# A rebuilt attention stage in a tokenizer, attention and expert kernel: two 34-row projections side by side, decays moved, rows normalised after the gather

## The reference

```python
# tok: frame differences, embedding, smoothing forwards and backwards (alpha 0.1), a linear layer
x_diff = concat([0, xt[:, 1:] - xt[:, :-1]])
x_emb = einsum('btc,dc->btd', x_diff, W_ve) + b_ve
h = ((ewma(x_emb) + flip(ewma(flip(x_emb)))) * 0.5) @ W_lin.T + b_lin
# attn: 8 heads of 16, gammas[h] = 1 - 2**(-5-h), no softmax
xn = layernorm(h)
q, k, v = (xn @ w.T + b for the three weights)
scores = einsum('bihd,bjhd->bhij', q, k) / 4 * (gammas ** (j - i) where j >= i, else 0)
h = h + silu(xn @ wg.T + bg) * einsum('bhij,bjhd->bihd', scores, v)
# ffn: expert choice, 8 experts, 1024 tokens each of 12000
x = layernorm(h); logits = x @ Wr; probs = softmax(logits, axis=0)
vals, idx = top_k(probs.T, 1024); selected = x[idx]
out_e = gelu(selected @ W1 + b1) @ W2 + b2
h = h + zeros.at[idx].add(vals * out_e)
```

## Time and profile before

| | us |
|---|---|
| runs of the kernel | 817.87, 820.11, 822.39 (median 820.11) |
| span of the profiled execution, first to last instruction | 815.7 |
| median of the runs less that span | 4.4 |
| PE, DVE, ACT, POOL busy | 617.2, 545.2, 250.4, 419.9 |
| stage 1, to the first instruction of the next block | 0 to 487.0 |
| stage 2 | 487.0 to 815.7 |

### The profile page before, as it was taken

One profiled execution on the slowest core, in us unless ns is written; L12 is line 12 of the kernel. 1 busy time (PEld: TensorE's weight loads), 2 busy tenths in 40 slices (PEclk: granted clock), 3 DMA queues, 4 the chain that ended last, 5 costly groups with the idle time before them and its releaser, 6 DMA issues. The chain is left out here.

```text
span 815.7 us, 16774 instructions
## 1 busy us (share of the span) xinstructions
PE 617.2 (76%) x6179; PEld 452.2 (55%) x6179; DVE 545.2 (67%) x1422; ACT 250.4 (31%) x474; POOL 419.9 (51%) x329
## 2 busy tenths in 40 slices
PE   2778898888988898899888854433488768867870
PEld 1456676666766676667666533433275456645650
DVE  7677998999888888888796737787455414442110
ACT  1222343333333333333333003440223412432340
POOL 1235654566445644564455000000578888888875
PEclk9976999999888988898888655555688679868886
DMA  5000011100111011001100112000124243333332
GB/s 176 25 1 24 21 45 46 45 23 24 44 44 28 17 44 44 25 19 44 44 20 21 40 48 70 0 0 1 28 61 63 37 73 71 44 56 71 43 33 26
DMA packets 43853, 32.33 MB, mean 40 GB/s; under 512 B 5094, under 2 KB 39204, under 8 KB 43812
## 3 DMA queue, kind: packets, MB, share of 16 engines
q1 hardware_dynamic: 31972, 21.57, 9.4%
q0 software_dynamic: 11264, 8.66, 8.3%
q10 hardware_dynamic: 576, 1.54, 0.5%
HBM read 13.35 MB, written 18.02 MB: 38 GB/s over the span
## 5 line engine op out<-in xcount | busy, mean ns | idle before, releaser
L658 POOL TENSOR_TENSOR prob<-prob,cst 125x500 f32<-125x500 f32 x90 | 105.2, 1169 | 164.8 <-ACT prob L579 164.7
L1229 POOL DMA_INDIRECT out<-y,idx_add x64 | 112.4, 1757 | 17.7 <-issue 16.7
L579 ACT COPY prob<-ps_score 125x500 f32<-125x500 f32 x90 | 51.9, 577 | 147.2 <-PE ps_score L382 145.0
L439 PE MATMUL bank<-xT,wT 128*128 128x375 f32 x192 | 84.7, 570 | 1.2 <-DVE q_dec L812 1.0
L1207 POOL DMA_INDIRECT taken<-rows_dram,idx x64 | 74.9, 1171 | 19.4 <-issue 18.1
L1123 PE MATMUL bank<-takenT,w_sb 128*128 128x512 f32 x128 | 74.5, 733 | 7.8 <-issue 7.8
L737 DVE TENSOR_TENSOR prob<-ps_score,cst 125x500 f32<-125x500 f32 x96 | 64.7, 674 | 21.9 <-PE ps_score L382 21.5
L663 POOL TENSOR_TENSOR rstd<-moments,cst 125x6 f32<-125x6 f32 x32 | 42.4, 1324 | 69.6 <-DVE moments L799 68.5
L403 PE MATMUL bank<-prob,v_split 125*32 125x125 f32 x1536 | 68.3, 301 | 0.0
L1196 POOL TENSOR_TENSOR carrier<-cst 1x1 f32<-1x1 f32 x25 | 11.9, 475 | 101.3 <-DVE idx L1383 98.0
L673 POOL TENSOR_TENSOR v_split<-v_tok,cst 125x768 f32<-125x768 f32 x32 | 58.2, 1819 | 7.0 <-DVE v_tok L855 7.0
(11 more groups left out here) (165 smaller groups left out, 1214.3 us busy)
## 6 DMA issues: line engine op xcount, KB each, us to landing
rows_dram<-row_sb SPq DMA_DIRECT2D x16, 398.4 KB
out<-h_sb SPq DMA_DIRECT2D x16, 375.0 KB
w_sb<-in_L_ffn_W SPq DMA_DIRECT2D x16, 256.0 KB
xin<-in_x ACTq DMA_DIRECT2D x4, 375.0 KB, 5.4
smooth_dram<-smooth SPq DMA_DIRECT2D x3, 375.0 KB, 2.4
s_in<-smooth_dram SPq DMA_DIRECT2D x12, 93.8 KB, 6.5
taken<-rows_dram,idx POOLq DMA_INDIRECT x64
out<-y,idx_add POOLq DMA_INDIRECT x64
```

What stands on the lines that cost most here:

```text
L439: pe.matmul(ps[:, 0:HALF * C], wT[:, w, :], xT[after.slot][:, k * HALF * C:(k + 1) * HALF * C], start=True, stop=True).then_inc(filled[f"{ ...
L658: pool.tensor_tensor(p, p, const("keep", C).unsqueeze(1).broadcast_to([C, H // 2, C]), ALU.mult).then_inc(high_masked, 1)
L1229: pool.indirect_dma_start(out=out_rows[:, :], out_offset=bass.IndirectOffsetOnAxis(ap=idx_add[it.slot][:, g:g + 1], axis=0), in_=y[it.slot ...
```

## The change

Stage 1 is written anew, all 18 steps unrolled, and stage 2 takes over one piece of it.

- **Norm 1 is folded.** For 4 items at a time (`LN_AT`, `SPREAD_AT`, `SMOOTH_AT`), the variance comes from the smoothed frames themselves (`norm_units`, `norm_products`, `variance_unit`), one power on POOL (`first_rstd`, 24 elements wide), is spread over rows by transposes, and multiplied into the 32 frames (`norm_rows`). The tile `e_in` holds 32 scaled frames, a row of rstd and a row of ones, twice: from row 0 and from row 64.
- **Projections** q, k, gate, k by tokens and v contract over these 34 rows, in pairs: one of a pair reads rows 0 to 33, the other rows 64 to 97. v comes out already split into even and odd heads.
- **Decays** sit in a full mask of 8x125 columns (instead of a broadcast triangle), in k by tokens, and in the gate (`decay_gate`, on POOL). q and k leave PSUM by plain copies on ACT.
- **States** are 32 columns for a pair of heads, 20 small matmuls, one product and one scan on DVE.
- **Residual and logits**: `output_units` adds h (33 rows, paired) and attn, each times [identity | router weights], in one PSUM group of 136 columns. ACT copies it to `row_sb`. There are no transposes of attn or of the row, no logits units and no h unit.
- **Norm 2** is not applied in stage 1: the row carries -mean*rstd and rstd (row of 138 values instead of 136), its logits are scaled by rstd, and in stage 2 ACT applies both to the gathered rows (`normalise`, 8 activations an expert) ahead of the transposes.
- **Transfers**: `smooth_dram` is gone. Each item has six loads inside SBUF (two of h's frames, two of the scaled frames, two of the rstd row), issued by SP behind the row write of an earlier item. The constants grow from 1031 to 1577 KB.
- `prob` has three buffers instead of two.

The core of the difference:

```diff
@@ SP @@
-            def step(n, before, own, after, coming):
-                if coming:
...
-                    sp.dma_start(s_in[coming.slot][0:CH, :], frames).then_inc(s_loaded[coming.slot], 16)
...
-                if before:
-                    sp.wait_ge(read["o1"], before.no + 1)
...
+            def load(it):
+                j, lo, slot = it // PER_BLOCK, it % PER_BLOCK * CH, it % PER_BLOCK
...
+                for at in (0, 64):
+                    sp.dma_start(r_in[slot][at:at + CH, :], smooth[mine, j, :]).then_inc(r_loaded[slot], 16)
+                sp.wait_ge(normed, 2 * j + 2)
+                sp.wait_ge(read["r1"], j + 1)
...
+                for at in (0, 64):
+                    sp.dma_start(e_in[slot][at:at + CH, :], s_norm[j % 2][mine, :]).then_inc(e_loaded[slot], 16)
+                    sp.dma_start(e_in[slot][at + CH:at + CH + 1, :],
+                                 rstd_rows[j % 2][lo:lo + 1, :]).then_inc(e_loaded[slot], 16)
+            def step(n, own, after, before):
+                if before is not None:
+                    slot = before % 2
+                    sp.wait_ge(read["o1"], before + 1)
...
+                    sp.wait_ge(row_done, before + 1)
+                    sp.dma_start(row_items[before:before + 1].rearrange("a p c d -> (a p) c d"),
+                                 row_sb[slot][:, :, :]).then_inc(rows_out[slot], 16)
+                if n + 2 < B:
+                    load(n + 2)
@@ PE @@
+            def feature_units(it, k):
+                slot = it % PER_BLOCK
+                if k == 0:
+                    pe.wait_ge(e_loaded[slot], (it // PER_BLOCK + 1) * 64)
+                for name, w, at in (("q", 0, 0), ("k", 1, 64)):
+                    ps = claim(f"{name}{k}", it)
+                    pe.matmul(ps[:, 0:HALF * C], w_raw[at:at + CH + 2, w, :], e_in[slot][at:at + CH + 2, half_of(k)],
+                              start=True, stop=True).then_inc(filled[f"{name}{k}"], 1)
...
+            def output_units(it):
...
+                for c in range(HALF):
+                    for k, at in enumerate((0, 64)):
+                        pe.matmul(ps[k][0:C, c * (D + E):(c + 1) * (D + E)],
+                                  r_in[slot][at:at + CH + 1, chunk(k * HALF + c)], h_w[at:at + CH + 1, :],
+                                  start=(c == 0), stop=False, skip_group_check=True)
+                pe.wait_ge(gated, chunk_no(it, 0) + 1)
...
+            def step(n, own, after, before):
+                if own is not None:
+                    scores(own, 4)
+                if after is not None:
+                    feature_units(after, 0)
+                if own is not None:
+                    values(own, 5)
+                    state_unit(own)
+                    scores(own, 3)
...
@@ DVE @@
+            def finish_rows(it):
+                row = row_sb[it % 2]
+                dve.wait_ge(rstd2_done, it + 1)
+                dve.scalar_tensor_tensor(row[:, :, MEAN_AT], moments2[:, :, 0], -1.0, row[:, :, RSTD_AT],
+                                         ALU.mult, ALU.mult)
+                dve.tensor_tensor(row[:, :, D:D + E], row[:, :, D:D + E],
+                                  row[:, :, RSTD_AT].unsqueeze(2).broadcast_to([C, NC, E]), ALU.mult
+                                  ).then_inc(row_done, 1)
@@ stage 2, ACT @@
+            def normalise(it):
+                for k in range(2):
+                    act.wait_ge(taken_in[it.slot][k], it.pair * 64 + 64)
+                    act.wait_ge(taken_turned, it.no * 2)
+                    for g in range(4 * k, 4 * k + 4):
+                        i = act.activation(takenN[:, g, :], taken[it.slot][:, g, 0:D], ACT.Identity,
+                                           bias=taken[it.slot][:, g, MEAN_AT:MEAN_AT + 1],
+                                           scale=taken[it.slot][:, g, RSTD_AT:RSTD_AT + 1])
+                    i.then_inc(taken_normed, 1)
```

More of the change, by code:

```diff
@@ new lines, in value_units @@
+            def value_units(it, ks):
+                ps = [claim(f"v{k}", it) for k in ks]
+                if it == 0 and ks[0] == 0:
+                    pe.wait_ge(values_weights, 2)
+                for half in range(2):
+                    for k, o in zip(ks, ps):
+                        at = 64 * (k % 2)
+                        m = pe.matmul(o[0:C, half * 2 * D:(half + 1) * 2 * D],
+                                      e_in[it % PER_BLOCK][at:at + CH + 2, chunk(NC - 2 - 2 * k + half)],
+                                      w_v[at:at + CH + 2, :, :].rearrange("p w d -> p (w d)"), start=True, stop=True)
+                        if half:
+                            m.then_inc(filled[f"v{k}"], 1)
@@ new lines, in _ @@
+            act.wait_ge(setup_pe, 4)
+            act.wait_ge(zeros_set, 1)
+            for g in range(4):
+                act.copy(a_blk[g * 32:(g + 1) * 32, g * 32:(g + 1) * 32], bank[1][g * 32:(g + 1) * 32, 0:CH])
+            act.activation(a_twice[:, :], bank[1][:, CH:CH + 1], ACT.Identity, scale=2.0)
+            act.activation(b_eps[:, :], bank[2][0:C, 0:1], ACT.Identity, bias=const("eps", C),
+                           scale=1.0 / D).then_inc(setup_act, 1)
+            act.wait_ge(setup_pe, 5)
@@ new lines, in rows, with gates @@
+            def rows(it, k):
+                if k == 0 and it >= 2:
+                    act.wait_ge(h2_out[it % 2], it // 2 * 16)
+                    act.wait_ge(rows_out[it % 2], it // 2 * 16)
+                act.wait_ge(filled[f"o{k}"], it + 1)
+                act.copy(row_sb[it % 2][:, k * HALF:(k + 1) * HALF, 0:D + E],
+                         bank_of(f"o{k}", it)[0:C, 0:HALF * (D + E)].rearrange("p (c d) -> p c d", d=D + E)
+                         ).then_inc(read[f"o{k}"], 1)
+            def gates(it):
+                if it >= 2:
+                    act.wait_ge(gated, (it - 1) * NC)
+                for k in range(2):
+                    act.wait_ge(filled[f"g{k}"], it + 1)
+                    act.activation(gate[it % 2][:, half_of(k)], bank_of(f"g{k}", it)[:, 0:HALF * C],
+                                   ACT.Silu).then_inc(read[f"g{k}"], 1)
@@ L702, in _ @@
-            all_steps(pool, step)
+            pool.memset(a_blk[:, :], 0.0).then_inc(zeros_set, 1)
+            fills = 1
+            for k in range(PER_BLOCK):
+                for part in (e_in[k][CH:CH + 2, :], e_in[k][64 + CH:64 + CH + 2, :], r_in[k][CH:CH + 1, :],
+                             r_in[k][64 + CH:64 + CH + 1, :]):
+                    pool.wait_ge(zeros_set, fills)
+                    pool.memset(part, 1.0).then_inc(zeros_set, 1)
+                    fills += 1
+            pool.wait_ge(zeros_set, fills)
@@ new lines, in _, with step @@
+            pool.wait_ge(values_weights, 2)
+            first_rstd(0)
+            def step(n, own, after, before):
+                if own is not None:
+                    high_mask(own, 4)
+                    high_mask(own, 3)
+                    high_mask(own, 2)
+                    high_mask(own, 1)
+                if n in LN_AT:
+                    first_rstd(LN_AT[n])
+                if before is not None:
+                    second_rstd(before)
+                if own is not None:
+                    high_mask(own, 0)
+                if after is not None:
+                    decay_gate(after)
+                    high_mask(after, 5)
```

1119 lines of the change are left out of this document (555 added, 564 removed).

## The result

The changed kernel takes **880.65 us** (median of 4, 875.55 to 886.25) against 818.99 us: ratio 1.078, interval 1.071 to 1.086. The forecast was 836. The profiled execution has a span of 878.0 us against 815.7.

What follows compares the result with a forecast made beforehand. PE's own work and the chain through the late loads bound it: cycle 16.8 + 3.4 + 1.2 + 7.4 = 28.8 us; stage 1 499 + stage 2 332.2 = 831, plus 4.4 gives 836 us; range 812 to 865.

Steps and rivals of the forecast that it cites:

- the wait: PE before an item's features, waiting for the six loads behind the row write: 5.9 us in each of 13 steps.
- the hold-up: SP's queue: the first transfer behind the row write takes 2.38 us instead of 0.51, within 7.4 to the landing.
- The pairs overlap: Two 34-row matmuls on PE run side by side; the rival without overlap had 896 us, chance 0.10.
- DVE is at a third: DVE's work per stage 1 item falls from 22.8 us to some 12, below 60% busy, and no longer bounds.
- The rival that had the wait short: Loads land in 5.3 us, cycle 24.4, time 779 us; chance 0.22 for cycles of 24 to 27.
- I take 8 us at the lower level, 3.4 lost: PE's clock after each wait in 13 steps: 8 us at the lower level, costing 3.4 us per cycle.
- the 44 us for steps 0 and 1: First two steps of stage 1, whose loads are early: 44 us together.
- the three of a block: Smoothing and norm of later blocks in stage 1: 2 x 5 = 10 us extra.
- PE's own work: PE's units for one stage 1 item: 19.5 us against 21.95 before, of which 16.8 in the cycle.
- an ordinary cycle: Stage 1, one item's features to the next's: 28.8 us against 27.2, thirteen making 374.
- stage 2: Grows by 3.5 us (0 to 8) from 328.65 to 332.2, for eight ACT activations per expert.
- a rival of 0.10: PE's clock does not come back in a step: cycle 38 us, time 956; chance 0.10.

Runs made afterwards that it cites:

- early-load kernel: Changed kernel with the six loads of item n+2 moved from behind the row write to the head of SP's step: 755.94 us.
- fills of 128 rows: Changed kernel with eight 128x128 matmuls of 375 columns, results overwritten, in PE's wait before the first features of items 3 to 15: 819.07 us.
- two pairs of fills: 128-row against 34-row matmuls, in the changed kernel's wait (819.07, 901.48 us) and in steps of a kernel with early loads and reordered work (724.23, 742.93 us).
- `e_in` first: Changed kernel with the four loads of `e_in` issued ahead of the two of `r_in`, still behind the row write: 865.69 us.
- 34-row fill: Changed kernel with eight matmuls of 34 rows of contraction filling PE's wait in items 3 to 15: 901.48 us.
- second run without stalls: Repeat of the kernel with early loads and smoothing sum and norm power reordered to remove two 1.85 us stalls: 725.20 us (first run 741.60).
- order alone: Changed kernel with early loads, two stalls removed by order, stage 2's second index matmuls earlier and first scaling halved, no fills: median 739.69 us, lower group 0.874.

## Why the prediction was wrong

**What held.** The place and the size of the wait. Forecast 5.9 us in 13 steps, measured 6.0 (77.6 in 13), released by the transfer of `e_in`. From the end of chunk 5's scores to the row write 1.0 (forecast 1.2), from there to PE's restart 8.0 to 8.5 (forecast 7.4; with the hold-up at the first `r_in`). That the mean is so close is in part luck: ordinary steps waited 6.4 to 7.0 us, because the loads took longer, and the first step and those behind a smoothing or a norm 4.5 to 5.6, because PE's last units ran at the lower level meanwhile. The pairs overlap. DVE is at a third. The rival that had the wait short fell.

**What failed: the clock.** The step was "I take 8 us at the lower level, 3.4 lost", and with it the 44 us for steps 0 and 1, which supposed that without a wait the clock is up. In the ordinary step from 142.52 to 172.50 it is 20.95 us from the features to the end of chunk 5's scores, where the early-load kernel takes 14.8 at the upper level: 6.1 lost, over 14.0 us at the lower level instead of 8. What this costs in all is shown by the fills of 128 rows, which leave the loads and the order as they are and keep the clock up through the wait: 819.07 us, 61.6 less than the changed kernel, where the forecast had 13 x 3.4 = 44. In the steps with smoothing and norm it is more, since the level goes down again within them, at 194 us in a stall of 1.86 us and at 225 us behind the variance unit with PE busy: the three of a block cost 10 us beyond three ordinary ones, where 5 were forecast. Steps 0 and 1, with no wait, took 57.5 us and were at the lower level but for 88 to 95 us.

**What hid a part of it.** PE's own work was put too high: 17.5 us an item instead of 19.5, of which 14.8 instead of 16.8 in the cycle. In the trace with the fills of 128 rows the state products take 0.6 instead of 1.3 (396.38 to 396.98), the outputs 2.5 instead of 2.85 (400.04 to 402.52). By that alone the time would have been 26 us lower.

The balance, forecast against trace: item 0's chunk 4 at 49.5 instead of 46 (+3.5); steps 0 and 1 57.5 instead of 44 (+13.5); from there to item 15's chunk 4, at 516.2, 409.2 instead of 384 (+25.2: an ordinary cycle 30.0 instead of 28.8, two blocks 20 instead of 10); the last two steps 22.7 instead of 25 (-2.3); stage 2 339.1 instead of 332.2 (+6.9); the median 2.65 above the span instead of 4.4 (-1.8). Together 45, from 836 to 881.

**Why the clock.** Row 470 of the earlier trace rows was there, with PE busy and the clock at 0.50 on small tiles, and I read it as a rival of 0.10 and no more. The runs show more. The change takes 128-row work out of the step: the projections and the transposes of `xn` and of the row went from 128 or 125 rows to 34, or away. In the changed kernel's stage 1 the clock came back fourteen times: ten times in the outputs or up to 3 us behind them, four times up to 3.5 us behind the norm's matmuls or transposes. Before, transposes of `xn` and `attn` and a projection stood right at the restart, and it was back after 5.7 us (231.38 to 237.1). That it matters which matmuls PE is busy with is shown by the two pairs of fills (82 and 19 us); rows of contraction are the difference by design, operands came along. That the loss of 128-row work is the reason why the changed kernel's clock comes back later is argued from where it rose, and not tried by itself.

**Stage 2** was mis-sized too: it grew by 10.5 us, with 13 for the scaling, and I had 3.5, with 8 as the bound. I counted eight activations a list at 0.3 us; they take 0.41, and in the first expert the two halves stood one behind the other ahead of PE, with the next list's index behind it.

**Left open.** Why the clock falls behind the variance unit in some steps and not in others (at 93 us in the kernel with early loads it stayed up): no run leaves the unit out. Nor is it known what decides between 714 and 740 us in executions of one program; the traces show only that the clock fell behind that unit in a slower one. And why the same step 0 came up at 61 us in two kernels (`e_in` first; the 34-row fill) and only at 86 to 89 in the others with the same start. So small tiles sometimes raise it; they don't do it reliably.

## What to carry to other kernels

A transfer that the next step asks for first belongs ahead of whatever its queue waits for at the end of a step: the loads at the head of the step were worth 125 us for two moved lines. When a change turns 128-row matmuls into small ones, price PE's work at both levels of the clock, and ask in each step what would bring the upper one back; stalls of 1 to 2 us can then cost several times their length. Read the clock from the duration of a unit that you know, beside the granted clock.

## What the runs showed of the hardware

- The clock fell while PE was busy: within a fill of 34-row matmuls (132 to 133 us), where one of 128-row matmuls kept it at 1.00; and behind the variance unit (186 and 285 us with early loads, 173 us in the second run without stalls, 95, 184 and 272 us with the order alone).
- Eight matmuls of 128 rows brought the clock back five times out of five; eight of 34 rows not once in five.
- A stall of 1.85 us in a step of small tiles was followed by 14 to 17 us at half speed, three times over, with early loads; the same kernel held the upper level without a stall from 321 to 400 us.
- Ahead of the first record of the clock, at 88 us, the granted clock reads 1.00, whatever the real level: 1.15 us for a chunk's scores at 58 us. The Trainium skill (the same page, Part 1) warns that a trace's clock events are not always to be trusted; here it is the stretch ahead of the first of them.
- The first issue behind the row write takes 2.4 to 2.6 us instead of 0.5, for `r_in` and for `e_in` alike.
- A power on 24 elements takes 4.16 us on POOL, on 6 elements 1.33.
